# Attention kernel, one core: a tile's probability product placed between the two units of the next tile's scores

## The chip, the cores and the metric

The kernel runs on one core of a Trainium2 chip. The metric is the device time of one launch in microseconds (us), lower is better.

## The reference

Input `x` is 4 x 1024 x 512 (batch, sequence, width) in fp32. The work is one attention layer and one linear layer, each followed by a layer norm of the residual sum. Cut to what matters here:

```
q, k, v = x @ Wq.T, x @ Wk.T, x @ Wv.T         # 32 heads of 16
q, k    = rope(q), rope(k)
scores  = q @ k.T / 4 + bias(i - j)            # bias only for 0 <= i - j < 256
scores  = where(i >= j, scores, -inf)
m       = max(rowmax(scores), offset[head])
p       = exp(scores - m)
out     = (p @ v) / (sum(p) + exp(offset - m))
x       = layernorm(x + out @ Wo.T)
x       = layernorm(x + quantised(x) @ quantised(Wff).T + bff)
```

## The kernel before

The kernel has three stages. The first projects q, k and v, rotates q and k and stores them in parts. The second is the attention, and the change lies in it. The third computes the output projection, both layer norms and the quantised linear layer.

The attention goes over 8 groups of 4 heads (`groups`, L450), and in each group over the 4 batches. One group and one batch are a **pair**, numbered n; there are 32 pairs. In a pair the scores are held transposed, keys on the partitions and queries along the free dimension, in 12 **tiles** T (L58, `tile_cols`). The queries are cut into two chunks c of 512, the keys into blocks J of 128. Chunk 0 has the tiles 0 to 3, of 512, 384, 256 and 128 columns; chunk 1 has the tiles 4 to 11, of which the first five have 512 columns, and the last three 384, 256 and 128. Each tile has two **units** u = 2T and 2T+1, of two heads each, so a pair has 24 units (NU). Ten of the tiles touch the bias band (`BANDED`); tiles 4 and 5 don't.

For each unit three engines work:

- TensorE computes the scores of its two heads (`scores`, L660, matmuls of L678) into one of two pairs of PSUM banks, chosen by u % 2. It may start when ScalarE has done the exponential of unit u-2 (wait on `exp_done`, L668). In an even unit of a banded tile TensorE also adds the bias, with two matmuls for each head (L684). In an odd unit of a banded tile the bias is already in the bank: ScalarE has put it there (`seed`, L928, instructions of L938 and L940), and TensorE waits for `seeded` (L675).
- ScalarE takes the exponential of the unit into `probs` (`exp_unit`, L918, L925), which has three buffers, one for each tile.
- When both units of a tile have their exponentials, TensorE multiplies the probabilities by v (`pv`, L690, matmuls of L699: four heads in four column tiles of 32, shown as 8 instructions for a product). The product adds into one bank, `ps_o`. It waits for the exponential of the tile's second unit (L693). The first product of a chunk, of tile 0 or tile 4 (J = 0), also waits until ScalarE has copied out what the chunk before left in `ps_o` (`o_copied`, L697).

ScalarE's own order is written out in `phase2` (L964). After the exponential of each odd unit comes the seed for the next tile, if that is banded. The copy of `ps_o` (`copy_out`, L950, L952) for chunk 1 of the pair before stands behind the exponential and the seed of unit 1 (EVAC_LEFT), and the copy for chunk 0 behind the exponential of unit 9 (EVAC_0). At a pair's end ScalarE also issues a small exponential, L957.

Between these, TensorE and VectorE work ahead for the pair two further on. The row maxima need the scores a second time, in the other orientation: `maxima` (L648, matmuls of L657) writes into a ring of three PSUM banks, and VectorE reads them (L1158, L1165). A pair has 48 such matmuls, spread over the units (`units_beside`, L101): one inside a unit, between its two heads, and one or two behind it. A few transposes stand at fixed units as well: one of the shifts at unit 1 (L715), and one of the output at units 4 and 13 (L708).

Each engine runs its own instructions in the order in which they are written. TensorE's order is that of `phase2` (L767 to L799), which the change touches. The product of tile T stands there behind the scores of unit 2T+3, that is, behind both units of tile T+1. The last product of a pair, of tile 11, stands behind unit 1 of the next pair (PV_LEFT = 1), and in the very last pair at its end (L798). The sync engine issues the loads: the next v waits for all the products of the pair before (L600).

Of the kernel before, what the change touches and what calls it, by code (L numbers as in the profile page):

```python
# [63 lines left out]
def tile_cols(T):  # L64
    c, J = TILES[T]
    i0 = max(P * J, CH * c)
    return c, J, i0, CH * (c + 1) - i0


def band_cols(T):  # L70

    c, J, i0, w = tile_cols(T)
    b0 = i0 - P * J
    return b0, max(0, min(BAND - b0, w))
# [26 lines left out]
def units_beside(u):  # L101

    ks = list(range(min(NM, NM * u // SPREAD), min(NM, NM * (u + 1) // SPREAD)))
    return ks[:1], ks[1:]

PV_LEFT, EVAC_LEFT, OT_LEFT = 1, 1, 4
EVAC_0, OT_0, MT_LEFT = 9, 13, 1

W_UNITS = (6, 8, 10, 12)
# [91 lines left out]
def ahead(g, b, k=AHEAD):  # L203

    return (g, b + k) if b + k < B else (g + 1, b + k - B)
# [7 lines left out]
def slot_free(k, depth):  # L213

    return FIRST + k - depth + 1
# [27 lines left out]
def build(nc, hT, h, wqT, wkT, wvT, woT, bias, bias_rev, offset, wff, bff, cos, sin, out):  # L243
    ctx = ExitStack()
    with ctx:
# [209 lines left out]
        def before_in(g, b):  # L455
            return (g, b - 1) if b else (g - 1, B - 1)
# [181 lines left out]
        def _(pe):  # L638
# [4 lines left out]
            def wait_use(use):  # L643

                if not isinstance(use.before, int) or use.before >= RING:
                    pe.wait_ge(ring_read, use.before - RING + 1)

            def maxima(g, b, ks, use_of):  # L648

                for k in ks:  # L650
                    I, c0, c1 = MAX_UNITS[k % NMU]
                    hl = k // NMU
                    if k == 0:
                        pe.wait_ge(stack_loaded[b], 16 * 9 * (g + 1))
                    use = use_of(k)
                    wait_use(use)
                    pe.matmul(ps_ring[:, use.bank, 0:c1 - c0], q_stack[0:STACK, b, hl, I * P:(I + 1) * P],  # L657
                              k_stack[0:STACK, b, hl, c0:c1], start=True, stop=True).then_inc(ring_filled, 1)

            def scores(g, b, n, u, between):  # L660

                c, J, i0, w = tile_cols(u // 2)
                if u == 0:
                    if isinstance(n, int) and n == 3:
                        pe.wait_ge(ones_set, 5)
                    pe.wait_ge(shift_loaded[b], 16 * PARTS * (g + 1))
                    pe.wait_ge(bias_split, 3 * (g + 1))
                pe.wait_ge(exp_done, slot_free(n * NU + u, 2))  # L668
                b0, bw = band_cols(u // 2)

                in_bank = bw and u % 2
                if in_bank:
                    pe.wait_ge(seeded, n * NBAND + BANDED.index(u // 2) + 1)  # L675
                for hh in range(2):
                    hl = 2 * (u % 2) + hh
                    mm = pe.matmul(ps_s[:, u % 2, hh, 0:w], k_stack[0:ROWS, b, hl, J * P:(J + 1) * P],  # L678
                                   q_stack[0:ROWS, b, hl, i0:i0 + w], start=not in_bank,
                                   stop=bool(in_bank or not bw), skip_group_check=bool(in_bank))  # L680
                    if bw and not in_bank:
                        for s in range(2):
                            rhs = bias_r[:, bass.ds(g % 2, 1), s, hl, b0:b0 + bw].rearrange("p a c -> p (a c)")
                            mm = pe.matmul(ps_s[:, u % 2, hh, 0:bw], ident_r[:, :], rhs,  # L684
                                           start=False, stop=(s == 1))
                    if hh == 0:
                        between()
                mm.then_inc(scored, 1)

            def pv(g, b, n, T):  # L690

                c, J, i0, w = tile_cols(T)
                pe.wait_ge(exp_done, FIRST + n * NU + 2 * T + 2)  # L693
                if T == 0:
                    pe.wait_ge(v_loaded[b % 2], 16 * (g * 2 + b // 2 + 1))
                if J == 0:
                    pe.wait_ge(o_copied, FIRST + n * 2 + c)  # L697
                for hl in range(HG):
                    mm = pe.matmul(ps_o[VW * hl:VW * (hl + 1), i0 - CH * c:CH],  # L699
                                   v_sb[:, b % 2, J, VW * hl:VW * (hl + 1)], probs[:, T % 3, hl, 0:w],  # L700
                                   start=(J == 0), stop=(T + 1 in T_OF_CHUNK))
                mm.then_inc(pv_done, 1)

            def transpose_out(n, c, use):
                pe.wait_ge(o_copied, FIRST + n * 2 + c + 1)
                wait_use(use)
                for i in range(4):
                    mm = pe.transpose(ps_ring[:, use.bank, i * P:(i + 1) * P],  # L708
                                      o_sb[:, c, i * P:(i + 1) * P], ident[:, :])
                mm.then_inc(ring_filled, 1)  # L710

            def transpose_shift(n, use):
                pe.wait_ge(shift_steps, 4 * n + 2)
                wait_use(use)
                pe.transpose(ps_ring[0:HG * NB, use.bank, 0:P], shift[:, :], ident[:, :]).then_inc(ring_filled, 1)  # L715

            def transpose_weight(kt, use):
                pe.wait_ge(wq_steps, 24)
                wait_use(use)
                for nt in range(NK):  # L720
                    mm = pe.transpose(ps_ring[:, use.bank, :].bitcast(BF16)[:, nt * P:(nt + 1) * P],
                                      wq_nat[:, nt, kt * P:(kt + 1) * P], ident16[:, :])
                mm.then_inc(ring_filled, 1)
# [43 lines left out]
            def phase2(g, kind):  # L767
                last = kind == LAST_GROUP
                for b in range(B):
                    n = g * B + b  # L770
                    ga, ba = ahead(g, b)
                    more = not (last and b >= B - AHEAD)
                    left = b or kind != FIRST_GROUP

                    def use_of(what):
                        return Use(g, b, what, kind)

                    def use_before(what):
                        return Use(g, b - 1, what, kind)

                    for u in range(NU):
                        inner, behind = units_beside(u) if more else ((), ())
                        scores(g, b, n, u, lambda: maxima(ga, ba, inner, use_of))
                        if left and u == PV_LEFT:
                            pv(*before_in(g, b), n - 1, NT - 1)
                        if u % 2 and u > 1:
                            pv(g, b, n, u // 2 - 1)
                        maxima(ga, ba, behind, use_of)
                        if u == MT_LEFT and not (last and b > B - AHEAD):
                            transpose_shift(n + 1, use_before("M"))  # L790
                        if left and u == OT_LEFT:
                            transpose_out(n - 1, 1, use_before("O1"))
                        if u == OT_0:
                            transpose_out(n, 0, use_of("O0"))
                        if last and b == B - 1 and u in W_UNITS:
                            transpose_weight(W_UNITS.index(u), use_of(f"W{W_UNITS.index(u)}"))
                    if last and b == B - 1:
                        pv(g, b, n, NT - 1)  # L798
                        transpose_out(n, 1, use_of("O1"))  # L799

            groups(pe, phase2)


# [731 lines left out]
```

## Time and profile before

| | |
|---|---|
| time, median of 3 runs | 1770.17 us (1764.86 to 1771.36) |
| time of the profiled execution | 1767.04 us |
| its span, first to last instruction | 1765.2 us |
| TensorE matmuls busy | 1640.3 us, 93% |
| VectorE busy | 1280.5 us, 73% |
| ScalarE busy | 1087.4 us, 62% |
| GpSimd busy | 212.0 us, 12% |
| first and last exponential of L925 start at | 390.5 us and 1481.7 us |
| mean granted TensorE clock | 0.965 of full speed |

So the attention stage takes about 1092 us of the span. The ends of matmuls are modelled in the trace and overlap the next matmul's start, so TensorE's busy share says little about short gaps: they are read from the starts of consecutive matmuls. In the timeline, a row may stand for several instructions of a kind (x2, x8); its first number is the start and its second the time from the first one's start to the last one's end.

### The profile page before, as it was taken

Reading aid. Unit: us, or ns where it says so; the run is one execution under the profiler, and the core shown is the slowest. Engines: PE = TensorE matmul, PEld = TensorE weight load, DVE = VectorE, ACT = ScalarE, POOL = GpSimd, SP = SyncE. Lnnn points to the kernel's source line nnn. Section 1 sums busy time; section 2 is a strip of 40 time slices with the busy share of each in tenths; the row PEclk is TensorE's granted clock in tenths of the full one; section 3 lists DMA queues with packets and bytes.
Section 4 is the critical chain, followed back from the end, with each engine's and each line's share of the span. In section 5 each row is a group of like instructions: output and inputs, shape, how many; then the busy total and the mean of one; then the engine's idle time right before and its main releaser. Section 6 shows DMA issues by size and latency. Waiting matters only on the chain. (4 is left out here: it accounts for less than half of the span.)

```text
span 1765.2 us, 27891 instructions
## 1 busy us (share of the span) xinstructions
PE 1640.3 (93%) x9158; PEld 764.5 (43%) x9168; DVE 1280.5 (73%) x3812; ACT 1087.4 (62%) x1576; POOL 212.0 (12%) x109
## 2 busy tenths in 40 slices
PE   7999899889999999999999999999999998878773
PEld 3444344334444444444444444444444444433331
DVE  2454667568788888878888888888888872777776
ACT  2333233237877888787788878788887886333332
POOL 4323323230000000000000000000000000222222
PEclk9999999989999999999999999999999999989795
DMA  5447363534533633543452443335334120112211
GB/s 213 143 152 214 135 179 126 143 120 79 104 49 63 121 49 49 111 72 49 97 85 50 85 77 70 81 64 87 81 54 72 39 85 4 61 56 72 72 44 52
DMA packets 124501, 156.97 MB, mean 89 GB/s; under 512 B 14915, under 2 KB 80515, under 8 KB 124102
## 3 DMA queue, kind: packets, MB, share of 16 engines
q1 hardware_dynamic: 124358, 155.19, 38.1%
q8 instruction: 74, 1.21, 0.3%
q14 instruction: 69, 0.57, 0.1%
HBM read 103.90 MB, written 50.46 MB: 87 GB/s over the span
## 5 line engine op out<-in xcount | busy, mean ns | idle before, releaser
L925 ACT ACTIVATE probs<-ps 128x1024 f32<-128x1024 f32 (+3 forms) x768 | 592.3, 810 | 178.3 <-PE ps L684 119.3
L1165 DVE CUSTOM_DVE_ANT_0 junk<-ps,bias_q 128x384 bf16<-128x384 f32 (+2 forms) x1024 | 501.5, 502 | 137.3 <-PE ps L657 126.3
L657 PE MATMUL ps<-k_stack,q_stack 96*128 96x384 bf16 (+3 forms) x1536 | 492.8, 334 | 19.3 <-DVE mx L1165 12.0
L678 PE MATMUL ps<-q_stack,k_stack 99*128 99x512 bf16 (+3 forms) x1536 | 489.8, 328 | 18.7 <-ACT ps L940 10.4
L1158 DVE TENSOR_REDUCE mx<-ps 128x1 f32<-128x128 f32 (+3 forms) x768 | 365.2, 485 | 44.8 <-PE ps L657 37.1
L750 PE MATMUL ps<-attn 128*128 128x512 f32 x768 | 351.7, 602 | 10.5 <-DMA attn<-hT 9.3
L684 PE MATMUL ps<-bias_r,ident_r 128*128 128x384 f32 (+2 forms) x1280 | 352.3, 363 | 0.0
L699 PE MATMUL ps<-probs,v_sb 128*32 128x512 f32 (+3 forms) x3072 | 327.3, 498 | 0.1
L657 PEld LDWEIGHTS ps<-k_stack,q_stack 96*128 96x128 bf16 x1536 | 142.5, 97 | 373.9 <-DVE mx L1165 136.8
L684 PEld LDWEIGHTS ps<-bias_r,ident_r 128*128 128x128 f32 x1280 | 222.2, 192 | 36.9
L750 PEld LDWEIGHTS ps<-attn 128*128 128x128 f32 x768 | 144.9, 193 | 176.1 <-issue 163.7
L940 ACT ACTIVATE ps<-bias_s 128x768 f32<-128x768 f32 (+2 forms) x320 | 197.1, 616 | 22.5
L678 PEld LDWEIGHTS ps<-q_stack,k_stack 99*128 99x128 bf16 x1536 | 146.9, 98 | 102.6 <-issue 51.1
L823 PE MATMUL ps<-q_stack,k_stack 128*128 128x512 f32 x256 | 137.2, 689 | 43.0 <-DVE k_stack L1437 38.3
L1067 POOL TENSOR_TENSOR probs<-attn 128x1024 f32<-128x1024 f32 x32 | 105.3, 3292 | 257.2 <-ACT attn L884 182.9
L699 PEld LDWEIGHTS ps<-probs,v_sb 128*32 128x32 f32 x3072 | 60.6, 107 | 118.5 <-issue 96.6
L1243 DVE TENSOR_TENSOR probs<-attn 128x1024 f32<-128x1024 f32 x32 | 44.7, 1398 | 92.5 <-ACT attn L884 79.2
L1079 POOL CAST bias_r<-work 128x768 f32 (+1 forms) x8 | 6.6, 828 | 853.7 <-DMA work<-ext_k_dram 853.7
L823 PEld LDWEIGHTS ps<-q_stack,k_stack 128*128 128x128 f32 x256 | 55.4, 223 | 108.3 <-issue 99.8
L1165 DVE DVE_READ_ACCUMULATOR2_ANT mx<- 128x1 f32 x1024 | 84.1, 82 | 0.0
L893 ACT ACTIVATE v_sb<-ps 128x512 f32<-128x512 f32 x32 | 19.1, 598 | 103.4 <-PE ps L750 78.6
L938 ACT ACTIVATE ps<-zero 128x256 f32<-128x256 f32 (+2 forms) x128 | 70.0, 547 | 15.1 <-ACT probs L925 0.4
(103 smaller groups left out, 1004.1 us busy)
## 6 DMA issues: line engine op xcount, KB each, us to landing
q_stack<-q_parts SPq DMA_DIRECT2D x192, 128.0 KB, 4.3
v_dram<-v_sb SPq DMA_DIRECT2D x32, 512.0 KB, 2.8
v_sb<-v_dram SPq DMA_DIRECT2D x32, 512.0 KB, 9.8
k_stack<-k_parts SPq DMA_DIRECT2D x32, 384.0 KB, 7.3
q_parts<-q_stack SPq DMA_DIRECT2D x84, 128.0 KB, 2.0
k_parts<-k_stack SPq DMA_DIRECT2D x84, 128.0 KB, 2.0
attn<-hT SPq DMA_DIRECT2D x8, 1024.0 KB, 7.0
k_stack<-k_parts SPq DMA_DIRECT2D x32, 256.0 KB, 8.0
```

What stands on the lines that cost most here:

```text
L657: pe.matmul(ps_ring[:, use.bank, 0:c1 - c0], q_stack[0:STACK, b, hl, I * P:(I + 1) * P], k_stack[0:STACK, b, hl, c0:c1], start=True, stop= ...
L678: mm = pe.matmul(ps_s[:, u % 2, hh, 0:w], k_stack[0:ROWS, b, hl, J * P:(J + 1) * P], q_stack[0:ROWS, b, hl, i0:i0 + w], start=not in_bank, ...
L684: mm = pe.matmul(ps_s[:, u % 2, hh, 0:bw], ident_r[:, :], rhs, start=False, stop=(s == 1))
L699: mm = pe.matmul(ps_o[VW * hl:VW * (hl + 1), i0 - CH * c:CH], v_sb[:, b % 2, J, VW * hl:VW * (hl + 1)], probs[:, T % 3, hl, 0:w], start=(J ...
L750: mm = pe.matmul(ps[:, RING + tile % PBANKS, :], lhsT, rhs, start=(kt == 0), stop=(kt == NK - 1))
L823: mm = pe.matmul(ps_y[:, w, :], at_T[par][:, w, kt * P:(kt + 1) * P], wo_sb[:, kt, :], start=(kt == 0), stop=(kt == NK - 1))
L925: act.activation(probs[:, (u // 2) % 3, 2 * pr:2 * pr + 2, 0:w], ps_s[:, pr, :, 0:w], ACT.Exp).then_inc(exp_done, 1)
L938: act.activation(ps_s[:, 1, :, bw:w], zero[:, :].unsqueeze(2).broadcast_to([P, 2, w - bw]), ACT.Copy)
L940: act.activation(ps_s[:, 1:2, :, 0:bw], bias_s[:, bass.ds(g % 2, 1), :, b0:b0 + bw], ACT.Copy)\
L1067: pool.tensor_tensor(by_sin[:, q % 2, :, :], raw[:, q % 2, :, :], rope_cs[:, 1, q % 2, c:c + 1, :].broadcast_to([P, 2, CH]), ALU.mult).the ...
L1158: ins = dve.tensor_reduce(mx[:, par, hl, I, slot:slot + 1], ps_ring[:, use.bank, 0:far], AX.X, ALU.max)
L1165: ins = dve.tensor_tensor_reduce(out=junk[:, use.bank, 0:c1 - lo], in0=ps_ring[:, use.bank, lo - c0:c1 - c0], in1=bias_q[:, hl, BAND - t0 ...
```

## The change

Two lines change. The product of tile T moves from behind unit 2T+3 to behind unit 2T+2, between the two units of tile T+1. The last product of a pair moves from behind unit 1 of the next pair to behind its unit 0. Nothing is added or removed, and the orders of the other engines stay as they are.

```diff
-PV_LEFT, EVAC_LEFT, OT_LEFT = 1, 1, 4
+PV_LEFT, EVAC_LEFT, OT_LEFT = 0, 1, 4
...
                         scores(g, b, n, u, lambda: maxima(ga, ba, inner, use_of))
+
                         if left and u == PV_LEFT:
                             pv(*before_in(g, b), n - 1, NT - 1)
-                        if u % 2 and u > 1:
+                        if u % 2 == 0 and u:
                             pv(g, b, n, u // 2 - 1)
                         maxima(ga, ba, behind, use_of)
```

The order of TensorE's work, without maxima and transposes (S is a unit's scores, P a tile's product, ' marks the pair before):

```
before:  S0 S1 P11' S2 S3 P0 S4 S5 P1 ... S22 S23 P10
after:   S0 P11' S1 S2 P0 S3 S4 P1 S5 ... S22 P10 S23
```

## Rows read from the trace of the kernel before

**Rows 1.** The page's first part, and its row of the granted TensorE clock.

```profile
PE 1640.3 (93%) x9158; PEld 764.5 (43%) x9168; DVE 1280.5 (73%) x3812; ACT 1087.4 (62%) x1576; POOL 212.0 (12%) x109
...
PEclk9999999989999999999999999999999999989795
```

**Rows 2.** Busy time by stretch: PE, PEld, DVE, ACT, POOL, clock, DMA share, GB/s.

```profile
300.00:400.00 100.00, 85.34 (x241) 36.38 (x240) 64.21 (x134) 32.58 (x41) 27.18 (x8) 0.91 0.41 122
...
900.00:1000.00 100.00, 99.01 (x706) 47.80 (x704) 82.10 (x294) 79.59 (x120) 3.42 (x3) 1.00 0.42 77
...
1441.00:1482.00 41.00, 37.79 (x282) 16.82 (x280) 19.92 (x35) 36.80 (x55) 0.00 (x0) 1.00 0.08 27
```

**Rows 3.** Timeline of ScalarE over the start of pair 16.

```profile
940.12 0.66 ACT L925 ACTIVATE probs<-ps 128x256 f32<-128x256 f32 x2 [0.80 <-PE ps L684]
...
942.13 1.94 ACT L925 ACTIVATE probs<-ps 128x1024 f32<-128x1024 f32 x2
944.19 0.82 ACT L940 ACTIVATE ps<-bias_s 128x768 f32<-128x768 f32 x1
944.94 0.58 ACT L952 ACTIVATE o_sb<-ps 128x512 f32<-128x512 f32 x1
```

**Rows 4.** Timeline of TensorE's matmuls over the start of pair 16.

```profile
939.92 0.29 PE L678 MATMUL ps<-q_stack,k_stack 99*128 99x128 bf16 x2
940.14 0.64 PE L699 MATMUL ps<-probs,v_sb 128*32 128x256 f32 x8
940.71 0.39 PE L678 MATMUL ps<-q_stack,k_stack 99*128 99x512 bf16 x1
...
943.53 0.33 PE L678 MATMUL ps<-q_stack,k_stack 99*128 99x384 bf16 x1
...
944.70 0.34 PE L657 MATMUL ps<-k_stack,q_stack 96*128 96x384 bf16 x1
945.15 0.32 PE L678 MATMUL ps<-q_stack,k_stack 99*128 99x384 bf16 x1
...
945.73 1.07 PE L699 MATMUL ps<-probs,v_sb 128*32 128x512 f32 x8
946.73 0.34 PE L657 MATMUL ps<-k_stack,q_stack 96*128 96x384 bf16 x1
```

**Rows 5.** Timeline of ScalarE, same pair, from unit 8's exponential on.

```profile
953.18 1.94 ACT L925 ACTIVATE probs<-ps 128x1024 f32<-128x1024 f32 x2 [1.00 <-PE ps L678]
955.00 0.60 ACT L952 ACTIVATE o_sb<-ps 128x512 f32<-128x512 f32 x1
```

**Rows 6.** Timeline of TensorE's matmuls, same pair, units 8 to 13.

```profile
952.76 0.38 PE L678 MATMUL ps<-q_stack,k_stack 99*128 99x512 bf16 x1
...
953.53 0.38 PE L678 MATMUL ps<-q_stack,k_stack 99*128 99x512 bf16 x1
953.84 0.43 PE L699 MATMUL ps<-probs,v_sb 128*32 128x128 f32 x8
954.20 0.39 PE L657 MATMUL ps<-k_stack,q_stack 96*128 96x512 bf16 x1
...
955.03 0.74 PE L657 MATMUL ps<-k_stack,q_stack 96*128 96x512 bf16 x2
955.60 0.38 PE L678 MATMUL ps<-q_stack,k_stack 99*128 99x512 bf16 x1
...
956.22 1.07 PE L699 MATMUL ps<-probs,v_sb 128*32 128x512 f32 x8
957.22 0.28 PE L657 MATMUL ps<-k_stack,q_stack 96*128 96x256 bf16 x1
...
958.31 0.39 PE L657 MATMUL ps<-k_stack,q_stack 96*128 96x512 bf16 x1
958.82 0.38 PE L678 MATMUL ps<-q_stack,k_stack 99*128 99x512 bf16 x1
```

**Rows 7.** The page's row of the v loads: count, size, us to landing.

```profile
v_sb<-v_dram SPq DMA_DIRECT2D x32, 512.0 KB, 9.8
```

## The prediction

> **What bounds the kernel now.** I read the page first: TensorE's matmuls fill 93% of the span, VectorE 73%, ScalarE 62% [rows 1]. Then the busy time by stretch: in the steady part of the attention TensorE stands at 99%, VectorE at 82% and ScalarE at 80%, at the full granted clock [rows 2]. So TensorE's order sets the time of this stage, and neither of the others has much room: a wait of a microsecond on TensorE is not made up by anything. Last I read the timelines of TensorE and ScalarE of one pair side by side [rows 3 to 6], because the modelled ends of matmuls hide short waits. The reader is to see two things there.
>
> First, the waits of before that the change can remove. Unit 3's scores start at 945.15, the seed they need ended at 944.19 + 0.82 = 945.01, and the maximum's matmul ahead of them started at 944.70 and takes about 0.16 to the next start: TensorE stood for 0.29 us, and a wait on ScalarE costs 0.14 us from the end of the producer to the start of the matmul [rows 3, 4]. Unit 13's scores do the same: the maximum ahead started at 958.31 and needs 0.22, unit 13 starts at 958.82, 0.29 lost [rows 6]. In the other banded tiles the seed is there in time. These waits, some 0.6 us of about 34 us in a pair (1092 us over 32 pairs), are all that a better order can win.
>
> Second, where ScalarE copies out `ps_o`. The copy for the pair before stands behind the exponentials of units 0 and 1 and a seed: the chain from the start at 942.13 to the end at 944.94 + 0.58 = 945.52 has no idle time in it [rows 3], and product 0 starts at 945.73, right behind unit 3 and just 0.21 after the copy [rows 4]. So product 0 has no slack at all for going earlier. Product 4 starts at 956.22, 0.62 after the copy's end at 955.60 [rows 5, 6].
>
> **The change, part by part.** It moves 384 products and adds or removes nothing, so TensorE's own work stays; only waits can change. The engine executes matmuls in the order written, so all that stands behind a waiting product (a maximum's matmul, the odd unit's scores) waits too. What a product that has to wait for a copy costs is therefore the shift of its start, plus the work that stood ahead of it and now stands behind.
>
> *Start of a pair, 31 of 32 pairs* (the first has nothing to copy). Product 10, 0.57 us from its start to unit 0's [rows 4], now stands ahead of unit 23. The scores of unit 23 come 0.57 later, and its exponential slips by less, since so far it waited for the one before it: scores done at 940.21, exponential of both units from 940.12 to 940.78, of which the second half starts about 940.40 [rows 3, 4]. So it slips 0.38 to 0.57; I take 0.45. On ScalarE everything behind it follows without idle time, seed, small exponential, exponentials 0 and 1, seed and copy [rows 3], so the copy ends 0.45 later, at 945.97. Unit 0 and unit 1 with product 11 between them cost TensorE the same as before; the seed for unit 1 slips too, but exponential 1 queues behind exponential 0 and hides it. TensorE is through with unit 2 at about 944.8 and then stands until 945.97 + 0.14 = 946.11: a wait of 1.3 us in front of product 0. Against 945.73 the product starts 0.38 later. Behind it now stand a maximum's matmul (0.17) and unit 3 (945.15 to 945.73, 0.58 less some 0.1 for the change to the product's tiles): 0.65. Sum **+1.03 us**. The 0.29 wait of unit 3 is gone in this.
>
> *Change of chunk, all 32 pairs.* Product 3, 0.36 us, now stands ahead of unit 9 [rows 6]. Unit 9's second head starts 0.44 later, at 953.97. An exponential of this width starts 0.42 after its unit's second head (952.76 to 953.18) [rows 5, 6], so exponential 9 starts at 954.39 in place of 954.10: 0.29 later, and the copy with it, to 955.89. Product 4 starts at 956.03, 0.19 earlier than before, after a wait of 0.9 us. But the two maxima (955.03 to 955.60 before; 0.39 without their own wait on VectorE) and unit 11 (0.62, less 0.1) now stand behind it. Sum 0.39 + 0.53 - 0.17 = **+0.75 us** (0.17 to be cautious for the 0.19). Unit 11 is late by this, so product 5, which needs exponential 11 (0.42 + 1.02 after unit 11's second head, against about 1.3 of TensorE's work until then), waits some **+0.20**. Unit 13 now has a product ahead of it, which covers its seed: **-0.29** [rows 6].
>
> *The other products* now wait for the exponential of the unit just ahead of the last one, where they had a whole unit more. The trace of before has no such wait. From below it is 0: in banded tiles unit 2T+2 carries the bias and lasts about as long as the exponential. From above it is some 0.14 for each of the nine, one pass of the signal, 1.3 us for a pair. I take 0 and keep the 1.3 for the range.
>
> *Past the queues.* A product issues no DMA. The v load for the next pair waits for product 11, whose place moves by under a microsecond, lands in 9.8 us and is needed some 30 us later [rows 7]: nothing. VectorE gets the same maxima; its 18% idle time grows by TensorE's waits.
>
> *Sum.* A pair: 1.03 + 0.75 + 0.20 - 0.29 = 1.69 us. All: 31 x 1.03 + 32 x 0.66 = 53 us. The last two pairs have no maxima and ScalarE bounds them (36.8 of 41 us busy [rows 2]); they lose about the same, since the same two copies stand in the same chain. The profiled execution took 1767.04, so 1820; the median of the runs is 3 us higher. I say **1822 us**.
>
> **The rivals.**
>
> *It wins what it aims at (faster).* If the products had no copy to wait for, the order would hide the seeds: 0.29 + 0.29 + 0.1 (unit 1) a pair, 22 us, 1748. The place that decides is product 0: it would need the copy to end by 944.7 instead of 945.97. Ten of twelve products indeed have no copy to wait for; against it stands that ScalarE is without idle time between 942.13 and the copy's end [rows 3]. Chance 0.04. That it comes out within 0.5% (about what a measurement of this kernel can tell from no change, 9 us) needs the two losses to be a third of their size: 0.05.
>
> *Every product waits.* If the signal's 0.14 and more is paid at most tiles, because TensorE's and ScalarE's turns are no longer one unit apart, up to 1.3 us more a pair, 41 us: up to about 1863. For: units 18 to 22 are narrow and the bias short. Against: ScalarE is idle a fifth of the time. Chance 0.10 that it is more than half of this.
>
> *The clock falls.* Waits of over a microsecond twice in 34 us could let TensorE's clock drop to its lower level. In the stretch 300 to 400, where TensorE waited more, the granted mean was 0.91 [rows 2]. At 0.91 over the whole stage the time would be 1092 x (1/0.91 - 1) = 108 us more, about 1930. Against: in the last pairs TensorE is busy 37.8 of 41 us, with waits like these in every tile, and the clock there is 1.00 [rows 2]. Chance 0.03.
> The Trainium skill, in "TensorE: Matmul & The Clock Gate", section "A second HAM failure mode: psum-queue depth-cycling", says that short idle times between groups of matmuls, often enough repeated, make the clock swing between its two levels. By that rule this rival would be the likely one; the row of the last pairs speaks against it.
>
> *The forecast* gets the rest, 0.78.
>
> **How the numbers follow.** Forecast 0.78, more waits 0.10, clock 0.03, within 0.5% 0.05, faster 0.04; so slower 0.91. The range: low, the copies bind with less (slips 0.2 smaller, exponentials a little earlier: 1.1 us a pair), 1800; high, half of the other products' waits and 0.3 more at the copies, 1850. Beyond it lie the faster and even cases, the clock and a part of the second rival.
>
> **What the changed profile would show.** Product 0 and product 4 start 0.14 us behind the end of the copy of L952, in every pair, and TensorE's weight loads for L699 have idle time put down to L952, some 63 times, about 1.3 and 0.9 us each, 60 to 70 us in all; before there was none. TensorE's wait on the seed (L940) is gone except at unit 1. The busy share of TensorE falls to about 94% in the steady part, VectorE's and ScalarE's by 3 to 4 points; the clock stays 1.00. A pair takes about 35.8 us against 34.1. I am wrong if the products wait on exponentials (L925) for more than on the copies, if ScalarE reaches the copy earlier than now, or if the stage is no longer than before.

## The result, and the profile after

The change makes the kernel slower, and by more than twice what was forecast: 1893.38 us (median of 4 runs, 1886.12 to 1894.69) against 1769.63 for the kernel before in 4 runs (1764.86 to 1771.36). The ratio is 1.0695, 95% interval 1.0661 to 1.0730. The profiled execution took 1894.69 us, with a span of 1892.9.

In the code of the changed kernel all lines behind L783 are one higher: L925 is L926, L940 is L941, L952 is L953.

First the page of the changed kernel: the busy times, the clock, and the groups of matmuls that the change touches. Behind the bar stand busy time and mean ns of one, then the idle time of the engine just before them with what ended most of it.

```profile
PE 1674.1 (88%) x9168; PEld 774.4 (41%) x9168; DVE 1273.9 (67%) x3812; ACT 1097.2 (58%) x1576; POOL 211.9 (11%) x109
...
PEclk9999999989999999999999999999999999978885
...
L657 PE MATMUL ps<-k_stack,q_stack 96*128 96x384 bf16 (+3 forms) x1536 | 491.6, 332 | 51.2 <-DVE mx L1166 19.5
L678 PE MATMUL ps<-q_stack,k_stack 99*128 99x512 bf16 (+3 forms) x1536 | 480.7, 328 | 8.9 <-ACT ps L941 6.2
...
L699 PE MATMUL ps<-probs,v_sb 128*32 128x512 f32 (+3 forms) x3072 | 327.7, 498 | 65.2 <-ACT o_sb L953 63.3
```

The products (L699) have 65.2 us of idle time ahead of them; 63.3 of it is the wait for the copy of the product bank. That was forecast. What was not forecast is in the row of the maxima's matmuls (L657): they have 51.2 us of idle time, and what ends most of it is VectorE. Before, that group had 19.3.

Next, who waited for the copy, from the view of its line, and the busy times of a stretch in the steady part (PE, PEld, DVE, ACT, POOL, clock, DMA share, GB/s).

```profile
  PE ps L699: 63.3, 63
```

```profile
1000.00:1100.00 100.00, 90.38 (x634) 43.13 (x634) 73.21 (x268) 71.44 (x109) 3.41 (x3) 1.00 0.44 81
```

63 waits are 31 starts of a pair and 32 changes of chunk. Against 99.0, 82.1 and 79.6 of 100 us before [rows 2], TensorE, VectorE and ScalarE are busy 90.4, 73.2 and 71.4: all three wait more. The clock is 1.00 as before.

Now the start of pair 16 in the timelines, which answers to [rows 3] and [rows 4]. ScalarE:

```profile
1003.48 1.92 ACT L926 ACTIVATE probs<-ps 128x1024 f32<-128x1024 f32 x2
1005.52 0.82 ACT L941 ACTIVATE ps<-bias_s 128x768 f32<-128x768 f32 x1
1006.27 0.58 ACT L953 ACTIVATE o_sb<-ps 128x512 f32<-128x512 f32 x1
```

TensorE:

```profile
1004.54 0.34 PE L678 MATMUL ps<-q_stack,k_stack 99*128 99x384 bf16 x1
...
1006.99 1.07 PE L699 MATMUL ps<-probs,v_sb 128*32 128x512 f32 x8 [1.12 <-ACT o_sb L953]
1007.99 0.34 PE L657 MATMUL ps<-k_stack,q_stack 96*128 96x384 bf16 x1
1008.16 0.33 PE L678 MATMUL ps<-q_stack,k_stack 99*128 99x384 bf16 x1
```

The copy ends at 1006.27 + 0.58 = 1006.85 and product 0 starts 0.14 later. Only behind it come a maximum and unit 3, whose seed ended at 1006.34, long before.

**Where the time went.** The modelled ends of matmuls hide short waits, so I took them from the starts: for each kind of neighbours (which line, how many columns, which line behind it) the smallest usual distance of two starts over the stage, and what goes beyond it in each case, put down to what the later matmul waits for. "Ring" are the matmuls that write into the ring of three banks (maxima and transposes), "scores" wait for exponential and seed, "products" for copy and exponential. The stage is the time from the first to the last matmul of L678.

| us | stage | products wait | ring waits | scores wait |
|---|---|---|---|---|
| before | 1099.6 | 0.5 | 18.6 | 35.0 |
| changed | 1220.3 | 70.3 | 88.6 | 17.7 |
| difference | +120.7 | +69.8 | +70.0 | -17.3 |

The differences add up to 122.5 us, against the 120.7 by which the stage grew. Which distance is called the smallest usual one moves a figure of the table by up to 7 us, and the differences by 1 or 2. And the time from unit 0 to units 4, 8, 12, 16 and 20 and to the next pair's unit 0, mean over pairs 1 to 28, says where in a pair:

| us | 0 to 4 | 4 to 8 | 8 to 12 | 12 to 16 | 16 to 20 | 20 to next 0 | pair |
|---|---|---|---|---|---|---|---|
| before | 6.20 | 5.48 | 4.96 | 6.93 | 6.62 | 4.19 | 34.37 |
| changed | 7.22 | 6.07 | 6.29 | 7.18 | 7.01 | 4.53 | 38.31 |
| forecast | 7.23 | 5.48 | 5.71 | 6.84 | 6.62 | 4.19 | 36.06 |

The start of the pair comes out to 0.01 us. All the rest is longer than forecast. Taken unit by unit, the ring's waits aren't spread over all tiles. In the changed kernel they come at few places: about 0.7 us a pair at unit 5, 0.4 at each of units 13 and 17, 0.3 at each of units 6, 8 and 21, 0.2 at units 11 and 12, and next to nothing elsewhere (before: 0.3 at unit 6 and 0.1 at unit 10). At units 5, 16 and 21, and at unit 10 just ahead of 11, a unit brings three maxima in place of two (`units_beside`); at unit 13 the transposes of the output want a bank too; at unit 8 the scores between the maxima have been short. What the ring does is seen around unit 8, where no copy is waited for. TensorE:

```profile
1013.71 0.64 PE L699 MATMUL ps<-probs,v_sb 128*32 128x256 f32 x8
1014.28 0.34 PE L657 MATMUL ps<-k_stack,q_stack 96*128 96x384 bf16 x1
1014.45 0.22 PE L678 MATMUL ps<-q_stack,k_stack 99*128 99x128 bf16 x1
1014.51 0.38 PE L657 MATMUL ps<-k_stack,q_stack 96*128 96x512 bf16 x1
1014.73 0.22 PE L678 MATMUL ps<-q_stack,k_stack 99*128 99x128 bf16 x1
1014.79 0.27 PE L657 MATMUL ps<-k_stack,q_stack 96*128 96x256 bf16 x1
1014.90 0.38 PE L678 MATMUL ps<-q_stack,k_stack 99*128 99x512 bf16 x1
1015.43 0.34 PE L657 MATMUL ps<-k_stack,q_stack 96*128 96x384 bf16 x1
```

VectorE over the same time:

```profile
1014.29 0.08 DVE L1166 DVE_READ_ACCUMULATOR2_ANT mx<- 128x1 f32 x1
1014.80 0.56 DVE L1166 CUSTOM_DVE_ANT_0 junk<-ps,bias_q 128x384 bf16<-128x384 f32 x1 [0.43 <-PE ps L657]
1015.29 0.08 DVE L1166 DVE_READ_ACCUMULATOR2_ANT mx<- 128x1 f32 x1
1015.29 0.29 DVE L1159 TENSOR_REDUCE mx<-ps 128x1 f32<-128x128 f32 x1
```

While the product runs, VectorE empties the ring and stands idle for 0.43 us. Then three maxima fill all three banks within 0.8 us (starts 1014.28, 1014.51, 1014.79), because the units between them are short. The fourth needs the first bank again. VectorE is through with that at 1015.37, and the matmul starts at 1015.43, 0.31 later than the 0.22 us that unit 8's 512 columns take. Idle time on VectorE first, then a wait of TensorE on VectorE: the one does not make up for the other. Before, the product stood in the middle of such a row of maxima.

The Trainium skill, in "Perfetto Trace Analysis", section "Optimization Strategy", says that the same gap repeated on the engine that should be saturated can mean too few buffers for the next tile. The trace agrees as far as it goes: the gap comes at the fourth user of a ring of three. No run has a larger ring; the kernel's PSUM tensor has eight banks, and ring, scores and product take them all.

A last part is outside the stage: span less stage grows from 665.6 to 672.6 us. The third stage ran at a mean granted clock of 0.80 in place of 0.82 (mean of the last 287 and 280 us), and its matmuls of L824 took 722 ns in place of 689.

### The profile page after: what moved, and what is told of

It is laid out like the page before. It is cut to its first block, busy times and chain, and to the rows that moved or that the text cites. A ratio compares the mean times of both kernels' runs of the same rounds, so it can differ in the third digit from the quotient of the medians.

```text
span 1892.9 us, 27901 instructions
## 1 busy us (share of the span) xinstructions
PE 1674.1 (88%) x9168; PEld 774.4 (41%) x9168; DVE 1273.9 (67%) x3812; ACT 1097.2 (58%) x1576; POOL 211.9 (11%) x109
## 4 chain that ended last, share of the span: by engine, by line
PE 51%; issue 20%; DVE 11%; ACT 10%; POOL 6%; DMA 0%; ACTq 0%; POOLq 0%; DVEq 0%; SPq 0%
PE ps L699 15%; PE ps L657 11%; PE ps L678 7%; PE ps L824 7%; PE ps L684 6%; POOL probs L1068 5%; ACT probs L926 5%; DVE mx L1159 4%; DVE junk L1166 2%; ACT o_sb L953 2%; PE ps L846 1%; PE ps L708 1%; ACT ps L941 1%; DVE k_stack L1438 1%; ACT k_stack L986 1%
## 5 line engine op out<-in xcount | busy, mean ns | idle before, releaser
L926 ACT ACTIVATE probs<-ps 128x1024 f32<-128x1024 f32 (+3 forms) x768 | 614.3, 805 | 289.1 <-PE ps L678 251.3
L657 PE MATMUL ps<-k_stack,q_stack 96*128 96x384 bf16 (+3 forms) x1536 | 491.6, 332 | 51.2 <-DVE mx L1166 19.5
L678 PE MATMUL ps<-q_stack,k_stack 99*128 99x512 bf16 (+3 forms) x1536 | 480.7, 328 | 8.9 <-ACT ps L941 6.2
L699 PE MATMUL ps<-probs,v_sb 128*32 128x512 f32 (+3 forms) x3072 | 327.7, 498 | 65.2 <-ACT o_sb L953 63.3
L657 PEld LDWEIGHTS ps<-k_stack,q_stack 96*128 96x128 bf16 x1536 | 144.4, 97 | 441.3 <-DVE mx L1166 164.8
L941 ACT ACTIVATE ps<-bias_s 128x768 f32<-128x768 f32 (+2 forms) x320 | 197.2, 616 | 22.4
L678 PEld LDWEIGHTS ps<-q_stack,k_stack 99*128 99x128 bf16 x1536 | 145.5, 98 | 94.7 <-issue 23.8
L824 PE MATMUL ps<-q_stack,k_stack 128*128 128x512 f32 x256 | 144.7, 722 | 42.8 <-DVE k_stack L1438 38.3
L699 PEld LDWEIGHTS ps<-probs,v_sb 128*32 128x32 f32 x3072 | 62.3, 108 | 144.0 <-issue 78.8
L824 PEld LDWEIGHTS ps<-q_stack,k_stack 128*128 128x128 f32 x256 | 58.4, 235 | 112.6 <-issue 104.2
```

The source lines that it names most:

```text
L824: mm = pe.matmul(ps_y[:, w, :], at_T[par][:, w, kt * P:(kt + 1) * P], wo_sb[:, kt, :], start=(kt == 0), stop=(kt == NK - 1))
L926: act.activation(probs[:, (u // 2) % 3, 2 * pr:2 * pr + 2, 0:w], ps_s[:, pr, :, 0:w], ACT.Exp).then_inc(exp_done, 1)
L941: act.activation(ps_s[:, 1:2, :, 0:bw], bias_s[:, bass.ds(g % 2, 1), :, b0:b0 + bw], ACT.Copy)\
```

## The experiments

Theory A after the result: two causes of about 70 us each, the copies, and the maxima bunched behind a product with a ring of three. Theory B: the copies are the only cause, and the ring waits follow from their stalls.

**Less work for VectorE, in both orders.** A maximum reads at most 128 columns of each part, so the row maxima are taken over part of the scores; all else stays.

```diff
-                far = min(c1, band0) - c0
+                far = min(c1, band0, c0 + P) - c0
...
-                    lo = max(c0, band0)
+                    lo = max(c0, band0, c1 - P)
```

> The order of before, but VectorE reads at most 128 columns of each part of a maximum's scores (the row maxima are taken over fewer columns). In the trace of the changed kernel TensorE's maxima matmuls start late by about 70 us more than before, and the copies of the product bank cost about 70 us. Theory A (two causes: the copies, and VectorE emptying the ring of three banks too slowly once the maxima stand bunched behind a product): the small ring waits of before (about 18 us) go, so about 1750 us. Theory B (the copies are the only cause, the ring waits follow from them): the same for this kernel, 1745 to 1770.

> The changed order with the same smaller VectorE work. Theory A: the ring waits are gone, the copies stay: 50 to 60 us over cheap_before, so about 1805 us. Theory B: the loss does not depend on VectorE, so it stays some 120 us over cheap_before, about 1870 us.

Measured: 1751.49 us in the order of before (ratio 0.9932, interval 0.9907 to 0.9957) and 1825.47 in the changed order (1.0363, 1.0335 to 1.0391). The loss is 74 us instead of 124. By the starts, the products wait 73.2 us, about as in the changed kernel; the ring waits are 3.1 and 26.0 us, the scores' 40.1 and 21.4. So the copies' part does not depend on VectorE and the ring's does, as theory A has it. It was 20 us off in that 23 us of ring waits stay: a read of 128 columns still takes VectorE 0.29 us, and many maxima have two of them. Most of these waits come at unit 5, where two maxima stand behind one unit. The row of this kernel's page for the products, in the changed order:

```profile
L699 PE MATMUL ps<-probs,v_sb 128*32 128x512 f32 (+3 forms) x3072 | 328.2, 498 | 66.0 <-ACT o_sb L953 62.9
```

**Maxima ahead of the product.** In the changed order, the maxima that stand behind a unit go ahead of the product.

```diff
+                        maxima(ga, ba, behind, use_of)
                         if left and u == PV_LEFT:
...
                             pv(g, b, n, u // 2 - 1)
-                        maxima(ga, ba, behind, use_of)
```

> The changed order, but the maxima that stand behind a unit go ahead of the product in place of behind it. Theory A: the ring gets its work spread again and the maxima run in the shadow of the wait for the copy: 50 to 85 us less than the changed kernel, 1810 to 1840. Theory B: only the shadow, 0.17 + 0.39 us in a pair, 18 us less, about 1875.

Measured: 1829.42 us, ratio 1.0407 (1.0366 to 1.0448). The ring waits fall from 88.6 to 52.4 us and those of the products from 70.3 to 41.5, for the maxima now run while the copy is waited for. Theory B's 18 us are excluded. What stays of the ring's waits lies at units 5, 6, 8 and 10; from unit 11 on they are gone. At unit 5 two maxima still follow each other, and the product that stood ahead of them there is gone.

**Products 0 and 4 in their old place.**

```diff
-                        if u % 2 == 0 and u:
+                        if (u % 2 == 0 and u and u // 2 - 1 not in (0, 4)) or u in (3, 11):
                             pv(g, b, n, u // 2 - 1)
```

> The changed order, but products 0 and 4, the two that wait for a copy, stand where they stood before (behind units 3 and 11). Theory A: the waits for the copies go, the ring waits stay in the other ten tiles: 1820 to 1850. Theory B: all of the loss goes, 1755 to 1775, a little below before where the seeds are hidden.

Measured: 1836.75 us, ratio 1.0434 (1.0396 to 1.0471). The products wait 1.1 us in all, the ring 89.4: the copies' part is gone, and the ring's 88.6 stay within a microsecond. These rows of the page show it; the scores' row has the seed waits back, since units 3 and 11 no longer have a product ahead.

```profile
L657 PE MATMUL ps<-k_stack,q_stack 96*128 96x384 bf16 (+3 forms) x1536 | 497.0, 333 | 52.8 <-DVE mx L1159 16.5
L678 PE MATMUL ps<-q_stack,k_stack 99*128 99x512 bf16 (+3 forms) x1536 | 482.5, 328 | 23.2 <-ACT ps L941 19.7
L699 PE MATMUL ps<-probs,v_sb 128*32 128x512 f32 (+3 forms) x3072 | 327.3, 498 | 1.0 <-ACT probs L926 0.5
```

**The change in two halves.** Only PV_LEFT = 0 in the kernel before, and the changed kernel with PV_LEFT = 1.

```diff
-PV_LEFT, EVAC_LEFT, OT_LEFT = 1, 1, 4
+PV_LEFT, EVAC_LEFT, OT_LEFT = 0, 1, 4
```

```diff
-PV_LEFT, EVAC_LEFT, OT_LEFT = 0, 1, 4
+PV_LEFT, EVAC_LEFT, OT_LEFT = 1, 1, 4
```

> The kernel before with one part of the change: only the last product of a pair moves, from behind unit 1 to behind unit 0 of the next pair. Theory A: exponential 1 and with it seed 1 come up to 0.45 us later, and unit 3 already waits for that seed, so 0 to 0.45 us in 31 pairs: 1764 to 1780 on the scale of before at 1764. If the ring is hit here too (no maximum comes between unit 0 and the product), some 5 us more. This part explains at most a tenth of the loss.

> The changed kernel without that part: products 0 to 10 stand between the units, the last one stays behind unit 1. Theory A: nearly all of the loss, ratio 1.06 to 1.07.

Measured: 1.0034 (1.0009 to 1.0058) and 1.0705 (1.0658 to 1.0753). With the last product alone moved, unit 0 to unit 4 takes 6.45 us in place of 6.20 and all other stretches stay. All of the loss lies in the other eleven products. The parts don't add at the start of a pair: the last product costs 0.25 us alone and nothing beside the others, for with and without it the copy ends 5.24 us after unit 0's start.

**Copies one exponential earlier**, in the changed order.

```diff
-PV_LEFT, EVAC_LEFT, OT_LEFT = 0, 1, 4
-EVAC_0, OT_0, MT_LEFT = 9, 13, 1
+PV_LEFT, EVAC_LEFT, OT_LEFT = 0, 0, 4
+EVAC_0, OT_0, MT_LEFT = 8, 13, 1
```

> The changed order on TensorE, and ScalarE copies the product bank one exponential earlier: behind units 0 and 8. Theory A: product 0 then waits for exponential 1 and not for seed and copy, 0.9 us less; product 4 for exponential 9, 0.3 us less: 35 to 45 us less than the changed kernel, ratio 1.045 to 1.05; the ring waits of 88 us stay. If the copies were the whole cause it would come near 1.00.

Measured: 1848.2 us, ratio 1.0478 (1.0438 to 1.0518). The products wait 24.6 us in place of 70.3, now for exponentials, and the ring waits 88.5 us, as in the changed kernel. Unit 0 to unit 4 takes 6.17 us: the loss at the start of a pair is gone.

**Both remedies**, early copies and the maxima ahead: the two diffs above together.

> Both remedies: the copies one exponential earlier, and the maxima behind a unit ahead of the product. Theory A: the gains nearly add (65 us of the maxima ahead, of which some 18 were in the shadow of the waits, and 40 of the copies): ratio 1.01 to 1.03, product waits under 30 us and ring waits about 50 us. If the two causes were one, it would be no better than the maxima ahead alone (1.04).

Measured: 1803.63 us, ratio 1.0212 (1.0172 to 1.0251); products 4.0 us, ring 52.4. The gains nearly add: the two alone would make 1.019.

**Bunched maxima without moving a product.** In the order of before, the maxima behind a unit go ahead of the product. Beside it ran the changed order with products 0 and 4 in their old place and the maxima ahead, the two diffs for these together.

```diff
+                        maxima(ga, ba, behind, use_of)
                         if left and u == PV_LEFT:
...
                         if u % 2 and u > 1:
                             pv(g, b, n, u // 2 - 1)
-                        maxima(ga, ba, behind, use_of)
```

> The order of before for scores and products; only the maxima behind an odd unit go ahead of the product in place of behind it, so that three maxima stand within the two short score blocks. It has no new wait for a copy and none for an exponential. If bunching alone makes ring waits (theory A), they rise from 18 us to 40 or more, ratio 1.015 to 1.04. If ring waits come only where a product stands between the units (theory B), the ratio is 1.00.

> The changed order with both losses treated: products 0 and 4 in their old place, the maxima ahead of the product. Theory A: no product waits, ring waits about 50 us, seed waits about 40 us: ratio 1.01 to 1.03. If the ring waits were caused by the copies' stalls they would be back at 18 us and the ratio at 1.00.

Measured: 1.0230 (1.0183 to 1.0278) for the first, whose products wait 0.3 us and whose ring waits are 65.5 us; 1.0282 (1.0236 to 1.0328) for the second, which has both remedies for the changed order, with 1.1 and 66.1 us (50 were expected for the ring). So bunching makes ring waits by itself, with no product between units and no wait for a copy. In the first kernel they come at units 5, 11, 17 and 21, and at 5, 17 and 21 they are about as long as in the changed kernel. The second has the waits that stayed with the maxima ahead, and 0.35 us a pair more at unit 11, where product 4 is back and the maxima stand bunched ahead of it. TensorE's timeline of the first, just ahead of product 4:

```profile
979.02 0.23 PE L657 MATMUL ps<-k_stack,q_stack 96*128 96x128 bf16 x1
979.08 0.38 PE L678 MATMUL ps<-q_stack,k_stack 99*128 99x512 bf16 x1
979.62 0.28 PE L657 MATMUL ps<-k_stack,q_stack 96*128 96x256 bf16 x1 [0.15 <-DVE mx L1158]
```

0.54 us lie between the last two starts, where the 512 columns take 0.22.

**Product 5 alone between its units**, in the kernel before; it waits for no copy, and unit 13 has a seed wait to hide.

```diff
-                        if u % 2 and u > 1:
+                        if (u % 2 and u > 1 and u != 13) or u == 12:
```

The second kernel of this kind also puts the maximum behind unit 12 ahead of the product:

```diff
+                        if u == 12:
+                            maxima(ga, ba, behind, use_of)
+                            pv(g, b, n, 5)
...
-                        maxima(ga, ba, behind, use_of)
+                        if u != 12:
+                            maxima(ga, ba, behind, use_of)
```

> The kernel before, and of all the products only number 5 stands between its units (12 and 13): it waits for no copy, and behind it unit 13 waits 0.29 us for its seed. Theory A: that wait goes, 9 us in 32 pairs, less what the ring gives back since two maxima stand bunched behind it ahead of the transposes: 0.992 to 1.003.

> The same, with the maximum behind unit 12 ahead of the product. Theory A: the seed's 9 us without the ring's part: 0.992 to 1.000.

Measured: 1.0087 (1.0054 to 1.0121) and, with the maximum ahead of this product, 1.0098 (1.0063 to 1.0134). Both expectations missed. Units 12 to 16 take 7.35 and 7.36 us in place of 6.93. The two kernels lose the same in different ways. The timelines of the first show it. ScalarE:

```profile
962.20 1.02 ACT L925 ACTIVATE probs<-ps 128x1024 f32<-128x1024 f32 x1 [0.75 <-PE ps L678]
963.34 0.60 ACT L938 ACTIVATE ps<-zero 128x512 f32<-128x512 f32 x1
963.88 0.58 ACT L940 ACTIVATE ps<-bias_s 128x512 f32<-128x512 f32 x1
```

TensorE:

```profile
962.00 0.33 PE L657 MATMUL ps<-k_stack,q_stack 96*128 96x384 bf16 x1
962.57 0.63 PE L708 MATMUL ps<-ident,o_sb 128*128 128x128 f32 x4 [0.23 <-DVE mx L1165]
...
964.12 0.34 PE L657 MATMUL ps<-k_stack,q_stack 96*128 96x384 bf16 x1
964.61 0.38 PE L678 MATMUL ps<-q_stack,k_stack 99*128 99x512 bf16 x1
```

Unit 13 no longer waits, but its exponential starts late behind the product, and so does the seed behind it, which ends at 964.46. Unit 15 waits for that seed: it starts at 964.61, 0.32 after the maximum ahead of it is through. Between units 13 and 15 there is no product, because product 6 has kept its place. The other part is the ring's: the transposes behind unit 13 start 0.57 us after the maximum ahead of them, whose 384 columns take 0.17, so they wait 0.4 us for a bank. In the second kernel, with the maximum ahead of the product, that wait is gone, and the seed's is the longer for it:

```profile
963.04 0.34 PE L657 MATMUL ps<-k_stack,q_stack 96*128 96x384 bf16 x1
963.95 0.38 PE L678 MATMUL ps<-q_stack,k_stack 99*128 99x512 bf16 x1 [0.57 <-ACT ps L944]
```

Unit 15 starts there 0.91 us after the maximum ahead of it, a wait of 0.74, as much as the 0.40 and 0.32 of the first kernel together. So the late seed sets the loss in both. The wait has moved on by a tile and brought more with it.

**Three orders from what was learned**, to tell whether the losses are local. Product 0 or products 5 to 9, or both, stand between the units, each behind the maxima; product 10 keeps its place. With product 0, product 11 stands behind unit 0 of the next pair and the copy comes one exponential earlier. The diff is that of both; the kernel with products 5 to 9 alone keeps the constants of before and has `between = [5, 6, 7, 8, 9]`, the one with product 0 has `between = [0]`.

```diff
-PV_LEFT, EVAC_LEFT, OT_LEFT = 1, 1, 4
+PV_LEFT, EVAC_LEFT, OT_LEFT = 0, 0, 4
...
+                        between = [0, 5, 6, 7, 8, 9]
+                        T = u // 2 - 1
+                        first = (u % 2 == 0 and T in between) or (PV_LEFT == 0 and u == 0)
+                        if first:
+                            maxima(ga, ba, behind, use_of)
                         if left and u == PV_LEFT:
                             pv(*before_in(g, b), n - 1, NT - 1)
-                        if u % 2 and u > 1:
-                            pv(g, b, n, u // 2 - 1)
-                        maxima(ga, ba, behind, use_of)
+                        if u > 1 and (u % 2 == 0) == (T in between):
+                            pv(g, b, n, T)
+                        if not (first):
+                            maxima(ga, ba, behind, use_of)
```

> The kernel before, and only products 5 to 9 stand between the units, each behind the maxima. They wait for no copy, each odd unit from 13 to 21 has a product over its seed, and product 10 keeps its place so that exponential 23 does not slip. If waits add up by segment (theory A, local causes), units 12 to 16 take 6.64 to 6.84 us in place of 6.93 and the rest is as before: 3 to 9 us less, ratio 0.995 to 0.999. If a product between the units costs by itself (rival: the order cannot win anywhere), 1.005 or more, as with product 5 alone (1.009).

> The kernel before, and only the start of a pair is changed: product 11 behind unit 0, the copy behind exponential 0, product 0 between units 2 and 3 behind the maxima. With copies early and maxima ahead in the changed kernel the stretch from unit 0 to unit 4 took 6.06 us against 6.20 before. Theory A: 6.0 to 6.1 us here, at most 0.1 us lost behind it: 0 to 6 us less, ratio 0.996 to 1.000. Rival: 1.005 or more.

> Both of these. Theory A: the gains add, since the waits are local: 3 to 13 us less than before, ratio 0.992 to 0.998. Rival: 1.01 or more.

| | ratio, interval | 0 to 4 | 4 to 8 | 8 to 12 | 12 to 16 | 16 to 20 | 20 to next 0 |
|---|---|---|---|---|---|---|---|
| products 5 to 9 | 1.0028, 1.0013 to 1.0043 | 6.19 | 5.48 | 4.96 | 6.65 | 6.62 | 4.60 |
| product 0, 11 and the copy | 0.9971, 0.9951 to 0.9991 | 5.84 | 5.56 | 4.96 | 6.92 | 6.62 | 4.19 |
| both | 0.9963, 0.9950 to 0.9977 | 5.84 | 5.56 | 4.96 | 6.64 | 6.62 | 4.60 |

The losses are local: what one stretch wins or loses, it wins or loses in each kernel. Units 12 to 16 take 0.28 us less when product 6 moves with product 5, and the stretch behind unit 20 takes 0.41 more where product 10 does not move with product 9, the price that product 5 alone paid behind it: unit 23 waits for its seed. That end I had not counted, so the expectation for products 5 to 9 missed. The second and third kernels are faster than the kernel before by about 0.3 to 0.4%: 1761.23 and 1760.79 us against 1767.35, with both intervals below 1. Between the two no difference is shown. Units 0 to 4 take 5.84 us where 6.0 to 6.1 were expected, and 0.08 is lost behind them. In the start of pair 16 of the second one, product 0 waits for nothing. TensorE:

```profile
940.37 0.34 PE L657 MATMUL ps<-k_stack,q_stack 96*128 96x384 bf16 x1
940.64 1.06 PE L699 MATMUL ps<-probs,v_sb 128*32 128x512 f32 x8
941.64 0.34 PE L678 MATMUL ps<-q_stack,k_stack 99*128 99x384 bf16 x1
```

ScalarE:

```profile
938.81 0.59 ACT L958 ACTIVATE o_sb<-ps 128x512 f32<-128x512 f32 x1
939.29 1.03 ACT L931 ACTIVATE probs<-ps 128x1024 f32<-128x1024 f32 x1
940.44 0.81 ACT L946 ACTIVATE ps<-bias_s 128x768 f32<-128x768 f32 x1
```

The copy is over at 939.40, the exponential at 940.32, and the seed (until 941.25) lies under the product.

## Why the prediction was wrong

The direction and the first mechanism were right, the size was not: 53 us were worked out, and 124 came.

- *TensorE's order sets the time, a wait is not made up.* Right. The waits by the starts add up to the difference of the stage in the changed kernel within 2 us.
- *Start of a pair, +1.03 us.* Right, in its parts too. The stretch grew by 1.02. Counted from unit 0's start, the copy ends 0.43 us later than before (0.45 forecast) and product 0 starts 0.35 later (0.38 forecast), 0.14 behind the copy, after a wait of 1.2 us (1.3 forecast).
- *Change of chunk, +0.75.* The wait for the copy is as forecast (0.87 us of idle time against 0.9), but the stretch grew by 1.33. The copy ends 0.63 us later than before, counted from unit 8's start, and not 0.29, and product 4 starts 0.16 later and not 0.19 earlier, because unit 8 waits 0.3 us for the ring. TensorE comes late to the product by as much as the copy does, so the wait itself hit its number. With another 0.2 us at unit 11, the ring makes nearly all of the other 0.58.
- *Copies in all.* 63 waits and 60 to 70 us were forecast; 63 waits and 63.3 us came, at the products' matmuls and not at their weight loads.
- *Seeds of units 3 and 13, -0.29 each.* Right: the scores' waits fell by 17.3 us, 0.54 a pair.
- *The other products, 0.* Right: by the starts, products 0 and 4 have all but 3 us of the products' waits. The 70.3 us by the starts and the 63.3 us of idle time are nearly the same 63 waits, measured in two ways. The rival that made each product wait had a chance of 0.10 and did not happen.
- *Product 5, +0.20.* Wrong, a small term: it waited in 2 of 32 pairs and starts 0.34 us behind the end of exponential 11 on average. The ring's waits at units 11 and 12 stand ahead of it and give the exponential its time. Where VectorE has less to read and these waits are gone, it waits 0.1 us.
- *"VectorE gets the same maxima; its 18% idle time grows by TensorE's waits."* This is the step that failed: it puts the maxima's waits for a bank of the ring at nothing. I had counted that the maxima keep their number, not what stands between them. Before, a product stood in the middle of them and gave VectorE a microsecond to catch up; now it stands ahead of the three that follow each other fastest. The change took that spacing away. It cost 70.0 us, 2.2 a pair, at the places named above and not in every tile. Three kernels show it from three sides: less work for VectorE takes 63 of the 89 us of ring waits away, moving the two products off the copies takes none, and bunching the maxima in the old order brings 47 with nothing else changed.
- *The clock.* Rightly given little: from 400 us on the stage ran at a granted clock of 1.00, with over 120 us of waits in it more than before. The Trainium skill, in "TensorE: Matmul & The Clock Gate", section "A second HAM failure mode: psum-queue depth-cycling", tells of a kernel in which frequent short idle times between groups of matmuls make the clock swing between its two levels. Here it didn't swing, with waits of 1.2 and 0.9 us in every pair. Only the third stage, which the change does not touch, ran somewhat slower (0.80 against 0.82), which is about the 7 us outside the stage. I didn't test why.
- *The range* ended at 1850 because it priced only ScalarE's part from above. The ring's wait had no term, so it had no bound either. The signs I named to look for (busy 94%, a pair of 35.8 us) came out at 90% and 38.3 us, and that was the mark of a second cause.

## What to carry to other kernels

When an instruction moves on the engine that sets the time, count two distances: how much later its own wait is over than its new place (here two copies, with waits of 1.2 and 0.9 us), and how it spaced the work around it, which another engine takes from a ring of few buffers (here 2.2 us a pair, as much as the copies). A long instruction that needs nothing from that engine is its time to catch up; it belongs in the middle of the ring's users, not ahead of them. And such an order is a rhythm: where a row of moved products ended and the next one kept its place, the odd unit behind waited for its seed: 0.3 and 0.7 us a pair behind product 5 alone, 0.4 behind products 5 to 9, 0.2 behind product 0. The other end of the row of five cost nothing.

## What was not expected of the hardware

TensorE waited 18.6 us for the ring with VectorE busy 82% of the stage (the kernel before), and 88.6 us with VectorE busy 73% (the changed one): in this ring of three, the order counted and not the share. Maxima of at most two 128-column reads still made 26.0 us of waits with VectorE busy 48.8 of 100 us (900 to 1000 us of that run).
